# Batch 0's compressed projection copied on chip by halves, the scan moved ahead of the high powers, and the importance ahead of two router softmaxes

## The reference, cut to what matters

```python
xB = einsum('bsd,de->sbe', x, Bm)
h_final = scan(h -> h @ A + u, xB)                 # 256 steps, state of 64
h_proj = h_final @ W_imp.T
importance = softmax(einsum('bsd,bd->bs', x, h_proj), axis=-1)
token_pref = softmax(einsum('bsd,nd->bsn', x, W_router), axis=-1)   # the router, 64 neurons
neuron_w = einsum('bs,bsn->bn', importance, token_pref), normalised over n
shared_compress = einsum('bn,ndr->bdr', neuron_w, compress)         # 16 x 256 x 128
Q = einsum('bsd,bdr->bsr', x, shared_compress)
scores = einsum('bsr,nr->bsn', Q, K) / sqrt(128)
topk_scores, topk_idx = top_k(scores, 8)           # then a weighted sum of rows of V
```

## Time and profile before

| | us |
|---|---|
| three runs, median (lowest to highest) | 1408.79 (1408.34 to 1409.49) |
| the profiled execution, its own time | 1409.37 |
| its span | 1407.6 |
| PE busy | 1331.4 (95%) |
| DVE busy | 1094.4 (78%) |
| ACT busy | 718.5 (51%) |
| POOL busy | 729.6 (52%) |
| mean granted clock of TensorE | 0.978 |

### The profile page before, as it was taken

The page is one execution under the profiler, slowest core; times in us unless marked ns, Lnnn a source line. Parts: engine busy times, 40 slices in busy tenths (PEclk is TensorE's granted clock), DMA queues, the critical chain, the costliest instruction groups (busy, mean ns, idle before and its releaser), DMA issues.

```text
span 1407.6 us, 25199 instructions
## 1 busy us (share of the span) xinstructions
PE 1331.4 (95%) x9839; PEld 999.2 (71%) x9839; DVE 1094.4 (78%) x1627; ACT 718.5 (51%) x1377; POOL 729.6 (52%) x1009
## 2 busy tenths in 40 slices
PE   9765699999999999999999999999999998999898
PEld 4443576878777777777777778787868685867775
DVE  1449988888888888888888888888888875236567
ACT  1443355555555555555556464646464634336465
POOL 0514446565656565555656564647474746332434
PEclk9978899999999999999999999999999999999999
DMA  9461212131312121212121212121212251002412
GB/s 370 149 204 30 79 46 74 50 81 49 77 51 74 54 72 53 73 53 72 54 72 54 72 53 72 54 72 56 70 54 65 60 171 34 16 16 92 152 39 84
DMA packets 57020, 109.84 MB, mean 78 GB/s; under 512 B 9422, under 2 KB 37574, under 8 KB 55750
## 3 DMA queue, kind: packets, MB, share of 16 engines
q1 hardware_dynamic: 39814, 61.64, 14.8%
q0 software_dynamic: 14848, 41.96, 10.5%
q10 hardware_dynamic: 2240, 4.63, 0.9%
HBM read 98.24 MB, written 9.95 MB: 77 GB/s over the span
## 4 chain that ended last, share of the span: by engine, by line
PE 78%; DVE 14%; issue 2%; another core or an unknown queue 2%; ACT 1%; DMA 1%; POOL 1%; SPq 1%; POOLq 0%; ACTq 0%; DVEq 0%
PE side_bank L379 46%; PE score_bank L379 28%; DVE cand_val L1114 4%; DVE cand_idx L1115 4%; DVE x_sum L1138 2%; PE score_bank L735 2%; PE side_bank L735 1%; DMA sc_in<-shared_compress 1%; DVE dispatchedT L1270 1%; POOL exp L1361 1%; DVE den_recip L1163 0%; PE score_bank L588 0%; POOL v_rows L1332 0%; PE side_bank L530 0%
## 5 line engine op out<-in xcount | busy, mean ns | idle before, releaser
L879 ACT COPY score_row<-score_bank 128x512 f32<-128x512 f32 x512 | 299.8, 590 | 170.8 <-PE score_bank L379 101.8
L1332 POOL DMA_INDIRECT v_rows<-in_V,top_idx x256 | 249.1, 973 | 187.7 <-DVE top_idx L1128 105.4
L1114 DVE MAX8 cand_val<-score_row 128x8 f32<-128x2048 f32 x128 | 291.7, 2279 | 57.8 <-ACT score_row L879 57.8
L1361 POOL TENSOR_SCALAR exp<-exp,exp_bound 128x256 f32<-128x256 f32 x512 | 247.5, 500 | 111.2 <-ACT exp L891 109.1
L1115 DVE FIND_INDEX8 cand_idx<-cand_val,score_row 128x8 uint32<-128x2048 f32 x128 | 292.5, 2285 | 0.0
L379 PE MATMUL score_bank<-keysT_hi,qT_hi 128*128 128x512 f32 x512 | 219.1, 428 | 31.0 <-ACT score_row L879 28.2
L379 PE MATMUL score_bank<-keysT_lo,qT_hi 128*128 128x512 f32 x512 | 205.3, 401 | 0.0
L379 PE MATMUL score_bank<-keysT_hi,qT_lo 128*128 128x512 f32 x512 | 204.9, 400 | 0.0
L891 ACT ACTIVATE exp<-side_bank 128x512 f32<-128x512 f32 x256 | 139.1, 595 | 98.6 <-PE side_bank L379 98.5
L1138 DVE SCALAR_TENSOR_TENSOR x_sum<-v_rows,top_weight,x_sum 128x256 f32<-128x256 f32 x256 | 141.5, 553 | 9.3 <-DVE top_weight L1134 0.2
L379 PEld LDWEIGHTS score_bank<-keysT_hi,qT_hi 128*128 128x128 f32 x512 | 98.2, 192 | 70.1 <-ACT score_row L879 32.1
(11 more groups left out here) (200 smaller groups left out, 2256.0 us busy)
## 6 DMA issues: line engine op xcount, KB each, us to landing
kT<-den_scratch SPq DMA_DIRECT2D x62, 256.0 KB, 4.6
f_quads<-in_f POOLq DMA_DIRECT2D x32, 256.0 KB, 3.6
comp_then_wqkv_raw<-in_comp SPq DMA_DIRECT2D x6, 1024.0 KB, 18.2
xT_by_step<-in_xTs SPq DMA_DIRECT2D x4, 1024.0 KB, 9.2
keysT_raw<-in_KmT ACTq DMA_DIRECT2D x8, 512.0 KB, 11.1
xT_in<-in_xT SPq DMA_DIRECT2D x16, 256.0 KB
x_sum<-in_x SPq DMA_DIRECT2D x32, 128.0 KB, 2.2
ctxT_in<-in_ctxT SPq DMA_DIRECT2D x16, 256.0 KB
```

The lines of the kernel that those rows point to most:

```text
L879: nc.scalar.copy(srow[n // PER % 2][:, i * CB:(i + 1) * CB], scb[n % 3]).then_inc(sem("score_evac"), 1)
L1114: own(nc.vector.max(cv[:, tile, cs], srow[g % 2][:, :]))
L1332: pool.indirect_dma_start(out=vg[:, k, :], out_offset=None, in_=V_rows, in_offset=bass.IndirectOffsetOnAxis(ap=i8[:, tile, k:k + 1], axis=0))\
L1361: last = nc.gpsimd.tensor_scalar(ex[i % NEX][:, k, :], ex[i % NEX][:, k, :], ub[:, k, c:c + 1], E_LO, ALU.min, ALU.max)
```

## The change

It has six parts.

- **Batch 0's compression stays on chip.** In each half SP issues eight copies from `scs` straight to `sc_in` (one row of 2048 numbers to 16 rows of 128, 8 KB each), then the four stores. The load back of batch 0 and the wait for the stores ahead of the weights are gone, and `sc_stored` is waited for after the weights. Batch 0's `xT_in` is issued ahead of the compress matrix.
- **A new column order of the compress matrix**, laid out on the host, so that a quarter c of the rows holds 4096 neighbouring columns. A half of a row is then 8 KB in one run in DRAM, where it was four runs of 2 KB.
- `scs` lies over the k=1 half of `xT_by_step`. `main_ready` is now set by POOL, behind the stores and DVE's `sel_done`. PE no longer waits for it, and ACT waits ahead of score block 4.
- **PE's order.** Both bm_powers come before power(4), router(0) before power(5), scan1 between power(5) and power(7) with power(6) in its middle, router(1) behind it, and router(2) and router(3) one place later. router_transpose(2) moves behind the importance products.
- **DVE and ACT.** The importance maximum comes before router(2)'s softmax and the two sums, and its exponential before router_exp(2). ACT's eleven load issues come before router_out(1).
- **Fillers.** warm takes a bank. Three of them go in the powers, and 3, 5 and 10 are added behind router_transpose(3), the importance transpose and the compression.

```diff
-        scs = xs[:, 0, :, :, :].rearrange("p h b s -> p (h b s)")
+        scs = xs[:, 1, :, :, :].rearrange("p h b s -> p (h b s)")
-        scd_st = scd.rearrange("q (o g c w) -> o c q g w", o=2, g=4, c=4)
+        scd_st = scd.rearrange("q (c o w) -> o c q w", o=2, c=4)
...
+            sp.dma_start(xt[:, :, :], xT[:, :, 0:S]).then_inc(sem("xt_in"), 16)
             for g in range(NG_SC):
                 sp.dma_start(comp_at[g], comp[:, g * CH:(g + 1) * CH]).then_inc(sem(f"comp_in{g}"), 16)
             for half in range(2):
                 sp.wait_ge(sem("sc_act"), 2 * half + 2)
                 sp.wait_ge(sem("sc_dve"), 2 * half + 2)
                 for c in range(4):
+                    for k in range(KT):
+                        r = 32 * c + 16 * half
+                        sp.dma_start(sct[r:r + 16, k, :], scs[32 * c + k:32 * c + k + 1, half * CH:(half + 1) * CH])\
+                            .then_inc(sem("sct0_in"), 16)
+                for c in range(4):
                     sp.dma_start(scd_st[half, c], scs[32 * c:32 * c + 32, half * CH:(half + 1) * CH])\
                         .then_inc(sem("sc_stored"), 16)
-            sp.dma_start(xt[:, :, :], xT[:, :, 0:S]).then_inc(sem("xt_in"), 16)
-            sp.wait_ge(sem("sc_stored"), 16 * NG_SC)
-            sp.dma_start(sct[:, :, :], scd_v[0]).then_inc(sem("sct_in"), 16)
             for n, (w, i, k) in enumerate(WCHUNKS):
                 sp.dma_start(wraw[:, 1, i, k, :], w[:, k * INNER:(k + 1) * INNER]).then_inc(sem(f"w_in{n}"), 16)
             sp.dma_start(wo[:, :, :], Wo).then_inc(sem("wo_in"), 16)
+            sp.wait_ge(sem("sc_stored"), 16 * 8)
             sp.wait_ge(sem("main_ready"), 1)
...
             for r in range(4):
                 power(r)
-                warm(1 + r // 2)
+                if r < 3:
+                    warm(1, pp[0])
...
+            pe.wait_ge(sem("pow_evac"), 4)
+            bm_powers(0)
+            bm_powers(1)
             power(4)
-            bm_powers(0)
-            power(5)
-            bm_powers(1)
-            power(6)
             pe.wait_ge(sem("ba_evac"), 2)
             pe.wait_ge(sem("xs_in0"), 16)
             router(0)
+            power(5)
+            pe.wait_ge(sem("ba_evac"), 4)
+            for q in range(1, 4):
+                pe.wait_ge(sem(f"xs_in{q}"), 16)
+            scan(range(0, 8))
+            power(6)
+            scan(range(8, RAD)).then_inc(sem("pre_pe"), 1)
             power(7)
             router(1)
...
             router_transpose(0)
             pe.wait_ge(sem("pre_dve"), PRE_DVE["scan1_evac"])
+            pe.wait_ge(sem("pow_evac"), 8)
             (scan2)
-            router(3)
+            router(2)
             (hproj)
+            router(3)
             router_transpose(1)
-            router_transpose(2)
             (importance products)
+            router_transpose(2)
             router_transpose(3)
+            warm(3, pp[1])
             (importance transposes)
+            warm(5, pp[0])
             (neuron weights, then the compression)
+            warm(10, pp[0])
...
-            pe.wait_ge(sem("main_ready"), 1)
...
                 key = ("q", batch, 0)
-                need(pe, "sct_in", 16 * (batch + 1))
+                if batch == 0:
+                    need(pe, "sct0_in", 16 * 16)
+                need(pe, "sct_in", 16 * batch)
...
-            act.wait_ge(sem("main_ready"), 1)
                 need(act, "score_full", n + 1)
+                if n == PER:
+                    act.wait_ge(sem("main_ready"), 1)
...
-            for r in range(8):
+            for r in range(7):
                 power(r)
             (DVE copies scan1 out)
+            power(7)
...
             router(1)
+            dve.wait_ge(sem("pre_pe"), PRE_PE["imp_pe"])
+            nc.vector.tensor_reduce(imx[:, 0:1], pp[0][:, 0:S], AX, ALU.max, negate=True)\
+                .then_inc(sem("pre_dve"), 1)
             router(2)
             router_sum(0)
             router_sum(1)
-            dve.wait_ge(sem("pre_pe"), PRE_PE["imp_pe"])
-            nc.vector.tensor_reduce(imx[:, 0:1], pp[0][:, 0:S], AX, ALU.max, negate=True)\
-                .then_inc(sem("pre_dve"), 1)
...
-            dve.wait_ge(sem("sc_stored"), 16 * NG_SC)
-            last.then_inc(sem("main_ready"), 1)
+            last.then_inc(sem("sel_done"), 1)
...
-            pool.wait_ge(sem("main_ready"), 1)
+            pool.wait_ge(sem("sel_done"), 2)
+            pool.wait_ge(sem("sc_stored"), 16 * 8)
+            nc.gpsimd.memset(sel[:, 0, 0:16], 1.0).then_inc(sem("main_ready"), 1)
...
-        "comp": a["L0_attn_compress"].reshape(NC, KT, P * R).transpose(1, 0, 2).reshape(P, P * R),
+        "comp": a["L0_attn_compress"].reshape(NC, KT, 4, NG_SC, 512).transpose(1, 0, 3, 2, 4).reshape(P, P * R),
```

More of the change, by code:

```diff
@@ L385, in mm3, with warm @@
                 return mm(o, ll, rh, start=False, stop=last)
-            def warm(n):
+            def warm(n, bank):
                 for _ in range(n):
-                    mm(pp[0][:, 0:P], hm[:, 0, 0:4, :].rearrange("p b m -> p (b m)"),
+                    mm(bank[:, 0:P], hm[:, 0, 0:4, :].rearrange("p b m -> p (b m)"),
                        hm[:, 1, 0:4, :].rearrange("p b m -> p (b m)"))
@@ L426, in _ @@
             pe.wait_ge(sem("v_const"), 1)
-            warm(6)
+            warm(6, pp[0])
             pe.wait_ge(sem("A_in"), 32)
@@ L430, in _, with scan @@
                 power(r)
-                warm(1 + r // 2)
+                if r < 3:
+                    warm(1, pp[0])
+            def scan(steps):
+                for i in steps:
+                    for k in range(KT):
+                        last = mm(pp[0][k * SD:(k + 1) * SD, 0:B * RAD], ba[:, k, RAD - 1 - i, :],
+                                  xs_step[:, k, i // 8, i % 8, :, :], start=(i == 0), stop=(i == RAD - 1))
+                return last
             pe.wait_ge(sem("bmt_in"), 16)
             pe.wait_ge(sem("small_in"), 16 * 5)
+            pe.wait_ge(sem("pow_evac"), 4)
+            bm_powers(0)
+            bm_powers(1)
             power(4)
-            bm_powers(0)
-            power(5)
-            bm_powers(1)
-            power(6)
             pe.wait_ge(sem("ba_evac"), 2)
@@ L441, in _ @@
             router(0)
+            power(5)
[5 more added lines that the diff above has]
+            scan(range(8, RAD)).then_inc(sem("pre_pe"), 1)
             power(7)
-            pe.wait_ge(sem("xs_in1"), 16)
             router(1)
-            pe.wait_ge(sem("ba_evac"), 4)
-            pe.wait_ge(sem("xs_in2"), 16)
-            pe.wait_ge(sem("xs_in3"), 16)
-            for i in range(RAD):
-                for k in range(KT):
-                    last = mm(pp[0][k * SD:(k + 1) * SD, 0:B * RAD], ba[:, k, RAD - 1 - i, :],
-                              xs_step[:, k, i // 8, i % 8, :, :], start=(i == 0), stop=(i == RAD - 1))
-            last.then_inc(sem("pre_pe"), 1)
-            pe.wait_ge(sem("pow_evac"), 8)
-            router(2)
             router_transpose(0)
             pe.wait_ge(sem("pre_dve"), PRE_DVE["scan1_evac"])
+            pe.wait_ge(sem("pow_evac"), 8)
             for j in range(RAD):
@@ L835, in _ @@
             router_out(0)
-            router_out(1)
             act.wait_ge(sem("xs_in3"), 16)
@@ L841, in _ @@
                 act.dma_start(dst, src).then_inc(sem("main_const"), 16)
+            router_out(1)
             key_hi(0)
@@ L847, in _ @@
             router_exp(1)
-            router_exp(2)
             act.wait_ge(sem("pre_dve"), PRE_DVE["imp_max"])
@@ L851, in _ @@
                 .then_inc(sem("imp_exp"), 1)
+            router_exp(2)
             router_exp(3)
```

## The result

The changed kernel takes 1417.18 us (median of six runs, 1415.32 to 1419.61), against 1408.57 us for the kernel before, measured with it (six runs, 1403.74 to 1410.15). The ratio is 1.0062, with a 95% interval of 1.0046 to 1.0077. It is **slower by 0.6%**, which is outside the predicted range. The profiled execution took 1419.44 us, with a span of 1417.6.

What follows compares the result with a forecast made beforehand. DVE's third MAX8, gated by q(1) behind SP's queue, was taken to bound the kernel. Issues 13.0 - 10.8, backlog +0.8 and earlier start -1.75 gave +1.2: 1409.9 us against 1408.79, range 1405.4 to 1413.6.

Steps and rivals of the forecast that it cites:

- The mechanism: At DVE's third MAX8: the end shifts by the larger of q(0)'s shift less 1.43 and q(1)'s, forecast +1.2 us.
- the marks I gave for "slower": Signs in SP's queue that the result would be slower: copies at over 0.6 us or stores at over 0.9.
- the slow queue: Rival "SP's queue becomes the bound": 24 issues take 18.4 us instead of 10.8, shift +5.8, 1414.6 us; chance 0.15.
- the price of an issue: On SP's queue: 0.45 us a copy, 0.60 a store and 0.04 between issues.
- part 2: Part on SP's queue: 24 issues take 13.0 us instead of 10.8, giving q(0) -2.0 and q(1) +1.2.
- start of SP's stretch: SP's issues start at 63.95 instead of 65.70, 1.75 us earlier, from the neuron weights taking 4.8.
- growth of the 24 issues: SP's copies and stores take 13.0 us before the weights begin, where the old stretch took 10.8.
- backlog ahead of batch 1's `sc_in`: Second half's stores, 1 MB, still in the queues ahead of the weights, delaying q(1) by 0.8 us.
- The likeliest case: The forecast itself, +1.2 us at the third MAX8, spanning 1408.3 to 1411.4 us; chance 0.42.
- I take it as one for one: From DVE's third MAX8 at 98.24 to the end: any shift of it moves the end equally.
- The gain ahead of the compression: Up to the compression: importance ends at 45.8, `token_weight_diag` at 52.8, neuron weights take 4.8; compression ends at 66.6.
- The rule on the stores: Store drain: longer runs assumed to close half the 258 to 407 GB/s gap; the skill's rule, under 5%, adds 0.8 us.

Runs made afterwards that it cites:

- first and third groups: Follow-up runs a1 to a4 on one chip and d to a8 on a second; the kernel before took 1405.62 and 1405.04 us in them.
- d: The kernel before, unedited, profiled once more beside variants on the same chip: 1406.82 us (one run).
- a1: Changed kernel with batch 0's old layout, stores, load back and waits; new engine orders and fillers kept: 1404.21 us, ratio 0.9986 to the kernel before.
- a2: Changed kernel with the old orders of TensorE, DVE and ACT and the old fillers; copies, layout and waits kept: 1415.15 us, ratio 1.0063 to before.
- a4: Changed kernel with the second half's eight copies issued from ACT's queue instead of SP's: 1408.91 us, ratio 1.0018 to the kernel before.
- a8: Changed kernel without the three added groups of fillers (3, 5 and 10): 1413.05 us, ratio 1.0048 to the kernel before.
- first pair: The kernel before and the changed kernel as first measured together: 1408.57 and 1417.18 us, ratio 1.0062.
- second group: Follow-up runs b1 to a5 on the second chip; the kernel before took 1409.47 us in it.
- c: The changed kernel again, unedited, on the same chip as variants of it: 1416.70 us, ratio 1.0057 to the kernel before.
- a5: a1 with the weights' loads issued behind batch 1's `sc_in`: 1404.76 us, ratio 0.9968 to the kernel before.
- a3: Changed kernel with its six weight pieces and Wo issued behind batch 1's `sc_in`: 1403.92 us, ratio 0.9987 to the kernel before.
- a6: a4 with the weights' loads issued behind batch 1's `sc_in`: 1401.93 us, ratio 0.9979 to the kernel before.
- a7: a5 with the importance steps on DVE and ACT and router_transpose(2) on PE put back as before: 1398.88 us, ratio 0.9950 to the kernel before.
- b1_before: The kernel before, unedited, run for a second profile: 1409.92 us (one run).

## Why the prediction was wrong

**The mechanism held.** The sum was to be the larger of q(0)'s shift less 1.43 and q(1)'s shift. q(1) decided, batch 1's `sc_in` took 10.8 us to land as before (10.96 in the kernel before, from 81.16 to 92.12), DVE waited ahead of its third MAX8, and the new order shortened the way to the compression. Of the marks I gave for "slower", copies at over 0.6 came true by their mean (0.65, though fourteen of sixteen took 0.59), stores at over 0.9 did not (0.71). The issues grew by 6.4 us, past the 4.5 from which the slow queue was to decide.

**The step that failed is the price of an issue**, in part 2: "I take 0.45 for the copies, as they have fewer and simpler pieces". Term by term, in us of shift:

| term | forecast | measured | from |
|---|---|---|---|
| start of SP's stretch | -1.75 | -3.57 | 65.70 to 62.13 |
| growth of the 24 issues | +2.2 | +6.4 | 17.2 against 10.8 |
| backlog ahead of batch 1's `sc_in` | +0.8 | +1.15 | first weight issue to q(1): 16.74 against 15.59 |
| q(1) | +1.2 | +3.96 | 92.12 to 96.08 |
| q(0) | -2.0 | -0.72 | 78.39 to 77.67 |
| third MAX8 | +1.2 | +4.07 | 98.24 to 102.31 |

The growth was 4.2 short. The copies make 3.2 of that (5.04 and 5.99 for two halves, against 3.9 each), the stores 0.8 (2.98 against 2.6, twice), the gaps between blocks the rest. I picked a value between bounds by an argument about the shape of the transfer, when the nearest row, a small store at 0.54, said otherwise. With 0.54 the same sum gives +2.7, at the limit of what counts as slower, and with the 0.59 of nearly all copies +3.5. The likeliest case would then have been on the other side, at 1412.3 us.

**A second step failed with it:** "I take it as one for one", from the third MAX8 to the end. The right price alone would have given a time inside the stated range. What put the result outside is a loss behind the gate, to which the last paragraph of this section comes back; its cause stays open.

**The rival "SP's queue becomes the bound"** was right in kind. It had 0.60 a copy and 0.98 a store, 18.4 in all, and 1414.6 us. I gave it 0.15, and counted its ends as independent misfortunes instead of asking which of the two prices a row supports.

**The gain ahead of the compression was larger than forecast**, and covered a part of the loss. The clock rose during router(0) (2.53 for the work that took 3.68 at the low level), sooner than behind router(0) and a power, where I had it, and the importance products ended at 45.1 against 45.8. DVE's idle time ahead of the importance maximum is 2.21 against my estimate of 2.3, and `token_weight_diag` was ready at 51.99 against 52.8. The neuron weights took 3.75 in this profile and 4.8 in the forecast, which is within what the same stretch did in the other kernels. `main_ready` was set at 82.8 (near 81 forecast) and cost nothing. One reading was a slip: at the pace of the row with two fillers in 1.22, five take 3.0 us at the low clock, not 1.5. It had no effect, since they took 1.28 at the high clock.

**The rule on the stores.** The stores ran at 198 GB/s in 68 to 70, with the DMA engines at 0.94, and at 242 in 70 to 72 at 0.95, where the shorter runs had reached 258. Over all the packets of the stores the traces have 0.550 us for one of 8 KB and 0.128 for one of 2 KB, which is 238 and 256 GB/s on sixteen engines. My assumption that longer runs drain faster failed. By the rule of the Trainium skill, DMA: Bandwidth & Descriptors, section Bandwidth, they would gain under 5%, with a backlog of 1.6 for my 0.8; the measured 1.15 lies between the two, and the rate was below both.

**From the gate to the end.** One for one holds where it could be read cleanly: in the first and third groups, the span less the third MAX8 is 1307.6 to 1308.5 for d, a1, a2, a4 and a8, while the MAX8 itself moves over 10.3 us. It fails to carry the whole loss in the first pair and in the second group. There the difference is 1309.4 to 1311.3 for the kernel before and 1315.3 and 1312.1 for the changed one, so that 4.8 us at the gate became 8.6 and 7.2 in the medians. With the gate's 4.8 alone the forecast would have been 1413.6, the upper end of the range. The other 2.4 to 3.8 us are **not explained** by any run here; the profiles of a2 and a8, with the same copies, don't show them, and by the medians a8 loses 8.0 for 7.5 at the gate and a2 9.5 for 7.9 (against d's profile). The traces only place them. From the third MAX8 over 2048 keys to the thirteenth it takes 68.5 to 68.6 us in all ten profiles with the weights in their old place, the changed kernel's two among them. So nothing more is lost up to there, some 170 us into the span. Behind it, to the start of the last of the 128, the changed kernel's profile has 1053.5 from the third one and the three of the kernel before in these sets 1050.3 to 1051.1, and from there to the end 261.8 against 258.8 to 260.4. c has 1051.0 and 261.2. So the rest arises in the steady part (the turns over the batches) and behind it, where these executions also show the waits that the last section lists.

## What to carry to other kernels

Price a move in the queue of an issuing engine by the number of issues times the shortest issue of a comparable small transfer in the trace, and don't go below it because the transfer is small: with 8 KB per issue the queue was the cost here and the DMA engines were nearly idle (a share of 0.06). When a load waits behind a block of others in the same queue, look at the order of that queue first. Moving seven loads that nothing needed yet behind the one that was needed took the changed kernel from 0.6% slower to 0.1% faster. On the old path it was worth less, 0.18% between a1 and a5, with intervals that overlap; no run has it on the kernel before alone. And split a change with several parts before judging it: this one held a gain (the scan order and fillers), what is probably a small loss (importance first) and a large loss (the copies), whose sum looked like one verdict.

## What the runs showed of the hardware that was not expected

**Vector waits out GpSimd's subtraction.** The kernels with late weights (a3, a5, a6, a7) gain 1.5 to 2.1 us between the third MAX8 and the thirteenth, which my theory did not have. In the changed kernel, DVE's two steps with two inputs, and POOL's six subtractions (2.4 us each) beside them:

```profile
112.72 2.67 DVE L1136 TENSOR_TENSOR pos_onehot<-chunk_offset,top_pos 128x256 f32<-128x256 f32 x1
115.43 2.46 DVE L1138 TENSOR_TENSOR pos_onehot<-pos_onehot,cand_idx_f 128x256 f32<-128x256 f32 x1
```

```profile
103.31 14.30 POOL L1339 TENSOR_TENSOR wqkv_lo<-comp_then_wqkv_raw,wqkv_hi 128x1024 fp32r<-128x1024 f32 x6 [20.48 <-ACT wqkv_hi L875]
```

In a5, where POOL is done at 107.04:

```profile
104.66 2.66 DVE L1134 TENSOR_TENSOR pos_onehot<-chunk_offset,top_pos 128x256 f32<-128x256 f32 x1
107.35 0.42 DVE L1136 TENSOR_TENSOR pos_onehot<-pos_onehot,cand_idx_f 128x256 f32<-128x256 f32 x1
```

```profile
92.88 14.16 POOL L1335 TENSOR_TENSOR wqkv_lo<-comp_then_wqkv_raw,wqkv_hi 128x1024 fp32r<-128x1024 f32 x6 [28.15 <-ACT wqkv_hi L874]
```

The same step takes 0.42 alone and 2.46 beside POOL. The increase, 2.04, is nearly the length of one of POOL's instructions, not a slower rate. The Trainium skill, SBUF — State Buffer, section SBUF: two separate sides, states it so: a GpSimd instruction that reads SBUF and a Vector instruction with two SBUF inputs take turns at a shared port pair, and the loser stands still for the winner's whole instruction. The rows agree.

**Two patterns of the steady part.** In the first pair of kernels and in the second group, where the kernel before is near 1409, the list of waits of every profile holds rows like these, here of b1_before (us in total, times, longest):

```profile
ACT v L896 <- remote: 67.0, 14, 5.2
DVE den_recip L1163 <- remote: 54.7, 14, 4.6
```

In the two groups where it is near 1405 no profile has them. There the kernel before (d) shows:

```profile
ACT v L896 <- PE side_bank L379: 79.1, 64, 2.9
```

b1 and d are the same program on the same chip, so neither the kernel nor the chip makes the difference. The medians of the kernel before in their groups, 1409.47 and 1405.04, are further apart than several variants are from the kernel before, which is why only ratios within a group were used here. What makes the difference stays open, and no run tried it. The part of the loss that isn't explained was seen only in the sets near 1409.
